# One program for the linear attention and the feed-forward, 512 tokens at a time

## The chip, the cores and the metric

The kernel runs on one core of a Trainium2 chip. The time is that of one execution on the device, in microseconds; the median of the runs shown is 2300.51 us. The profile is of one execution, taken by the hardware profiler; its instants are counted from the first instruction (the span's start).

## What is computed

Two layers, each of three parts with a residual, on x of 32 x 64 tokens x 256, all in float32. The change touches the second and third part of layer 0:

```python
x = x + L0_xattn(ctx, layernorm(x))            # latent attention, untouched
x = x + L0_attn(layernorm(x))                  # linear attention
x = x + L0_ffn(layernorm(x))                   # gated feed-forward
x = x + L1_xattn(layernorm(x), ctx, ctx, mask) # from here on: the decoder, untouched
x = x + L1_attn(layernorm(x))
x = x + L1_ffn(layernorm(x))
```

The linear attention takes xn = layernorm(x), q = relu(xn Wq + bq), k = relu(xn Wk + bk), v = xn Wv + bv, and for each sequence of 64 tokens and each of 16 heads of width 16 the state k^T v and the sum of k. The context is q times the state over max(q times the sum, 1e-6). Then y = context + xn goes through a layer norm of its own with gamma and beta. The feed-forward is silu(h Wg) * (h Wu), then Wd, with 768 hidden columns and weights given as integers, which are scaled by 1/127.

## The kernel before

The 2048 tokens are 16 tiles of 128 (NT); a chunk (CH) is 512 tokens, four tiles, and there are four chunks (NCH). x lies in SBUF all the time as x_sb, one row a token. The program is a list of stages (STAGES): latent_attention, linear_attention, feed_forward, then the decoder. Each stage has one instruction stream for each engine, written out by hand, with semaphores between them; nothing reorders them. Between two stages stands end_stage: the semaphores are cleared and all engines meet at a barrier, so no work of a stage begins ahead of the end of the one before. DMAs are issued by SyncE at the head of each stage.

Both stages begin with NormTranspose: statistics of all 16 tiles on VectorE (gather, L107), seven small steps on all 16 columns (L109 to L117), the power -0.5 on GpSimd (L125), 16 normalised tiles on VectorE (L128), transposes on TensorE (L192) and copies on ScalarE (L205); the feed-forward also subtracts the rounded copy (L176) for a low part.

linear_attention then computes all queries (L280, ScalarE L331) and goes through the tiles in the order keys_values(0), then for each t: states(t), keys_values(t+1), contexts(t). A tile's matmuls are keys and values (L289), states (L300) and contexts (L312). Its vector work is the two bias additions (L350, L351), the masked states (L362, L364), and the denominators, the division and the addition of xn into y (L372 to L382). ScalarE has the Relu of the keys (L337). PSUM has one bank for keys and values, two for states, one for contexts. Behind the last tile stand the statistics of y (L107 again), the power, and the scaling of 16 tiles with gamma and rstd (L397, L401). GpSimd adds beta to x_sb in one instruction (L263).

feed_forward loads the integer weights, converts them on VectorE (L495, L497), rounds them to fp32r on ScalarE (L475, L478) and takes the low parts on GpSimd (L441, L443). A product is then three fp32r matmuls (PASSES: high times high, high times low, low times high), by product3 (L83). For each chunk and each of 6 groups of 128 hidden columns (NH): gate and up matmuls into two banks each, Silu on ScalarE (L485), the product on VectorE (L514), rounding on ScalarE (L489), the low part on VectorE (L516). Then down for four tiles (L468) into two banks, and the addition to x_sb on VectorE (L504).

In the attention TensorE waits as follows: states(t) for the keys and values of t in SBUF and for the states of t-1 to be read out; keys_values(t+1) for the values of t to be read out; contexts(t) for the masked states of t, and for y of t-1.

TileStats, the decoder's form of the statistics, works on four tiles (PER) at a time: L540, L547 to L555, L564. The decoder's first 512-column matmuls are at L845.

## Time and profile before

| | us |
|---|---|
| median of three runs | 2300.51 (2300.44 to 2300.74) |
| profiled execution | 2298.4 |
| its span | 2296.7 |
| start of linear_attention (first SyncE issue) | 911.72 |
| start of feed_forward (first SyncE issue) | 1030.22 |
| start of the decoder (first SyncE issue) | 1171.61 |

Over the whole span TensorE is busy for 2145.7 us (93%), VectorE 1202.0 (52%), ScalarE 1066.5 (46%), GpSimd 483.7 (21%). These shares are means over very different stages. The page's 40 slices of 57.4 us show it: in slices 16 to 19 (861 to 1091 us) TensorE's digits are 7, 8, 4 and 5, where nearly all others are 9, and the digit of the granted clock falls to 7 in two of them. So the stages have to be read one by one: the stretches give the engines' busy time and the granted clock (1.00 is 2.4 GHz, 0.50 is 1.2 GHz), the timeline gives the order of the instructions and what each waited for.

### The profile page before, as it was taken

The numbers are of one execution on the slowest core, as the hardware profiler recorded it, in microseconds if no ns is written. First come the engines' busy times: TensorE is split into PE (matmuls) and PEld (weight loads), VectorE is DVE, ScalarE is ACT, GpSimd is POOL, SyncE is SP. The second block draws the span as 40 slices with busy tenths as digits, with TensorE's granted clock in tenths as the row PEclk, the third lists the DMA queues.
The fourth block names the chain that finished last, engine by engine and source line by source line (L and its number), as shares of the span: only waits on it lengthen the run. The fifth ranks groups of instructions, "written<-read, shape, count | busy, mean of one in ns | idle before, by whom it ended". The sixth has DMA issues, their size and how long they took to land. (4 is left out here: it accounts for less than half of the span.)

```text
span 2296.7 us, 51145 instructions
## 1 busy us (share of the span) xinstructions
PE 2145.7 (93%) x21377; PEld 1876.0 (82%) x21377; DVE 1202.0 (52%) x3545; ACT 1066.5 (46%) x2411; POOL 483.7 (21%) x365
## 2 busy tenths in 40 slices
PE   6999999999999997845979999999999899999999
PEld 6888989898988896424857888878989889898898
DVE  6655555555555554485345778862786532313311
ACT  4545444545444543203226666653444344444443
POOL 1000000000000000102011212223454454545544
PEclk9999999999999998977989999998999999999999
DMA  4100000000000000000031111010101011011000
GB/s 138 29 20 15 20 15 20 15 20 20 15 20 15 20 2 21 4 11 31 1 102 30 31 30 30 12 39 1 56 1 38 1 38 37 1 38 37 1 10 28
DMA packets 48805, 58.12 MB, mean 25 GB/s; under 512 B 6529, under 2 KB 40129, under 8 KB 48449
## 3 DMA queue, kind: packets, MB, share of 16 engines
q1 hardware_dynamic: 48576, 54.85, 7.6%
q8 instruction: 171, 2.80, 0.5%
q14 instruction: 58, 0.47, 0.1%
HBM read 46.72 MB, written 2.10 MB: 21 GB/s over the span
## 5 line engine op out<-in xcount | busy, mean ns | idle before, releaser
L797 POOL TENSOR_TENSOR moe_h<-moe_hr,moe_h 128x512 fp32r<-128x512 f32 x256 | 361.4, 1412 | 428.0 <-ACT moe_hr L1109 428.0
L1108 ACT ACTIVATE moe_h<-bank,dec_b 128x512 fp32r<-128x512 f32 x256 | 176.4, 689 | 418.9 <-PE bank L83 415.8
L2092 DVE TENSOR_REDUCE lat_neg_max<-bank 128x1 f32<-128x320 f32 x256 | 113.6, 486 | 319.0 <-PE bank L1873 319.0
L83 PE MATMUL bank<-lat_wv,lat_kv_t 128*128 128x256 f32 (+1 forms) x1728 | 264.8, 303 | 10.3 <-ACT lat_v L1967 3.9
L83 PE MATMUL bank<-lat_kv_t,lat_wk 128*128 128x320 f32 x1536 | 256.3, 316 | 0.0
L83 PEld LDWEIGHTS bank<-lat_wv,lat_kv_t 128*128 128x128 f32 x1728 | 224.1, 190 | 33.7 <-ACT lat_v L1967 5.7
L83 PEld LDWEIGHTS bank<-lat_kv_t,lat_wk 128*128 128x128 f32 x1536 | 225.8, 188 | 0.1
L1463 DVE SCALAR_TENSOR_TENSOR x_sb<-bank,moe_xs,x_sb 128x256 f32<-128x256 f32 x96 | 39.8, 477 | 352.0 <-PE bank L966 351.9
L83 PE MATMUL bank<-dec_xt,dec_lo 128*128 128x512 f32 x512 | 202.6, 396 | 0.0
L1981 ACT ACTIVATE lat_p<-bank,lat_neg_max 128x320 f32<-128x320 f32 x256 | 137.0, 535 | 114.0 <-DVE lat_neg_max L2092 114.0
L1569 POOL TENSOR_TENSOR lat_rs_rstdc<-lat_rs_varc,lat_rs_halfc 128x4 f32<-128x4 f32 x16 | 16.2, 1014 | 765.8 <-DVE lat_rs_varc L1561 765.8
L966 PE MATMUL bank<-dec_hi,moe_h 128*128 128x256 f32 x1024 | 166.5, 285 | 9.0 <-DVEq L1489 6.1
L1109 ACT ACTIVATE moe_hr<-bank,dec_b 128x512 f32<-128x512 f32 x256 | 174.6, 682 | 0.0
L1967 ACT COPY lat_v<-bank 128x512 f32<-128x512 f32 x128 | 75.1, 587 | 211.0 <-PE bank L83 211.0
L966 PEld LDWEIGHTS bank<-dec_hi,moe_h 128*128 128x128 f32 x1024 | 151.0, 193 | 21.4 <-issue 6.5
L966 PE MATMUL bank<-moe_hi,moe_h 128*128 128x256 f32 x1024 | 163.9, 282 | 3.0 <-POOL moe_h L797 2.9
L966 PE MATMUL bank<-dec_lo,moe_h 128*128 128x256 f32 x1024 | 164.8, 283 | 0.0
L83 PE MATMUL bank<-dec_xt,dec_hi 128*128 128x512 f32 x512 | 163.2, 400 | 0.0
L966 PEld LDWEIGHTS bank<-moe_hi,moe_h 128*128 128x128 f32 x1024 | 148.5, 189 | 14.9 <-POOL moe_h L797 4.6
L83 PE MATMUL bank<-dec_xt,moe_hi 128*128 128x512 f32 x512 | 159.4, 392 | 0.0
L1062 ACT ACTIVATE att_p<-att_sc,att_low 128x256 f32<-128x256 f32 x256 | 113.2, 510 | 83.7 <-DVE att_low L1216 83.7
L966 PEld LDWEIGHTS bank<-dec_lo,moe_h 128*128 128x128 f32 x1024 | 140.5, 190 | 0.0
(316 smaller groups left out, 3954.3 us busy)
## 6 DMA issues: line engine op xcount, KB each, us to landing
raw_w<-in_L_ffn_W SPq DMA_DIRECT2D x16, 1024.0 KB, 6.5
lat_ctx_raw<-in_ctx SPq DMA_DIRECT2D x16, 512.0 KB, 4.1
att_ctx_raw<-in_ctx_turned SPq DMA_DIRECT2D x16, 512.0 KB, 3.8
lat_kv_t<-lat_lt SPq DMA_DIRECT2D x32, 128.0 KB, 2.2
out_x<-x_sb SPq DMA_DIRECT2D x4, 512.0 KB, 2.9
x_sb<-in_x SPq DMA_DIRECT2D x1, 1792.0 KB, 14.7
lat_xl_now<-lat_xl SPq DMA_DIRECT2D x7, 256.0 KB, 4.5
lat_raw<-in_L_xattn_Wq SPq DMA_DIRECT2D x1, 1024.0 KB, 7.5
```

The source lines that it names most:

```text
L83: mm = pe.matmul(out, lhs(a, k), rhs(b, k), start=first and k == 0 and n == 0, stop=last and k == KD - 1 and n == 2)
L797: pool.tensor_tensor(h[:, g % 2, 1, :], hr[:, g % 2, :], h[:, g % 2, 0, :].bitcast(F32), ALU.subtract).then_inc(h_lo, 1)
L966: mm = pe.matmul(y_bank[c % 2 * 2 + i // 2][:, i % 2 * D:(i % 2 + 1) * D], h[:, n % 2, b, i * P:(i + 1) * P], w2(e % 2, a)[:, at, :], star ...
L1062: act.activation(p[:, m, r, :], sc[:, m, r, :], ACT.Exp, bias=low[:, m, r:r + 1], scale=-1.0).then_inc(p_ready, 1)
L1108: act.activation(h[:, n % 2, 0, :], h_bank[n % 2][:, :], ACT.Relu, bias=bias).then_inc(h_hi, 1)
L1109: act.activation(hr[:, n % 2, :], h_bank[n % 2][:, :], ACT.Relu, bias=bias).then_inc(h_f, 1)
L1463: dve.scalar_tensor_tensor(out=x_sb[:, t, :], in0=src(t), scalar=xs[:, t, e:e + 1], in1=x_sb[:, t, :], op0=ALU.mult, op1=ALU.add).then_inc ...
L1569: pool.tensor_tensor(self.rstd[:, :], self.vareps[:, :], self.half[:, :], ALU.pow).then_inc(self.rstd_ready, 1)
L1967: act.copy(v[:, vp % 2, 2 * b:2 * b + 2, :].rearrange("p t n -> p (t n)"), bank_of("v", c, off, a)[:, :]).then_inc(v_done, 1)
L1981: act.activation(p[:, hp % 2, h * LK:(h + 1) * LK], s_bank[h][:, 0:LK], ACT.Exp, bias=neg_max[:, u:u + 1], accum_out=rsum[:, u:u + 1]).the ...
L2092: dve.tensor_reduce(neg_max[:, u:u + 1], s_bank[h][:, 0:LK], AX.X, ALU.max, negate=True).then_inc(s_max, 1)
```

## The change

linear_attention and feed_forward become one stage, linear_feed; one barrier goes. Work goes by chunks of 512 tokens, and the feed-forward of chunk c-1 stands between the pieces of the attention of chunk c:

- TensorE: for each piece i of 0 to 4 a gate/up pair of the chunk before (gate_up), contexts of tile i-1, states of tile i, keys and values of tile i+1; then the sixth pair, the next chunk's transposes and queries, and the four downs, with the next keys and the transposes for this chunk's feed-forward between them. Chunk 0's attention has no feed-forward beside it, and the feed-forward of chunk 3 stands alone at the end.
- The eight PSUM banks are shared out anew: one for gate, one for up (before: two each), two for down, one for keys and values, two for states, which serve both kinds of transposes and the queries too, one for contexts.
- Statistics by TileStats, four tiles at a time, three of them (l, y, f). The normalised tiles are now made on ScalarE (Identity with scale rstd and bias shift, where shift is -mean times rstd, a new small multiply on GpSimd) instead of VectorE. Each chunk's transposes go four to a bank, with copies and subtractions of 512 columns.
- The integer weights are converted on GpSimd instead of VectorE (two tensor_scalar instructions); the low parts stay on GpSimd. All of it stands in one queue with the powers and with beta, which is added four tiles at a time. The weights' DMAs are issued at the head of the merged stage behind those of the attention.
- down waits for all six low parts at its first tile (before: one by one).

The order of each engine, cut (first the statistics, then GpSimd, TensorE, ScalarE, VectorE):

```diff
-        self.half = tools.sb("st_half" + tag, [P, n])
+class TileStats:
+
+
+
+    PER = 4
+
+    def __init__(self, tools, stats, rstd_ready, tag, double=False, minus=False):
+        self.raw = tools.sb("ts_raw" + tag, [P, NT, 6])
+        self.tmp = tools.sb("ts_tmp" + tag, [P, 5, NT])
+        self.mean = tools.sb("ts_mean" + tag, [P, NT])
+        self.vareps = tools.sb("ts_var" + tag, [P, NT])
+        self.rstd = tools.sb("ts_rstd" + tag, [P, NT])
+        self.half = tools.sb("ts_half" + tag, [P, NT])
         self.stats, self.rstd_ready = stats, rstd_ready
-        self.steps = n + 7
-
-    def gather(self, dve, row, base):
-
-        n, raw, tmp = self.n, self.raw, self.tmp
-        for t in range(n):
-            dve.bn_stats(raw[:, t, :], row(t)).then_inc(self.stats, 1)
-        dve.wait_ge(self.stats, base + n)
+        self.steps = self.PER + 7
+        self.half_sum = -0.5 if minus else 0.5
+        self.gain, self.bias = (1.0 + EPS, EPS * EPS) if double else (1.0, EPS)
+
+    def row(self, dve, src, t):
+        dve.bn_stats(self.raw[:, t, :], src).then_inc(self.stats, 1)
+
...
+        dve.tensor_scalar(tmp[:, 4, :], tmp[:, 2, :], self.gain / D, self.bias, ALU.mult, ALU.add).then_inc(self.stats, 1)
+        dve.wait_ge(self.stats, base + 6)
+        dve.scalar_tensor_tensor(out=self.vareps[:, at], in0=tmp[:, 3, :], scalar=0.25 * self.gain, in1=tmp[:, 4, :],
                                  op0=ALU.mult, op1=ALU.add).then_inc(self.stats, 1)
 
...
+            def power_and_shift(norm, shift, ready, c):
+
+                at = slice(c * PER, (c + 1) * PER)
+                norm.power(pool, c)
+                pool.wait_ge(norm.rstd_ready, c + 1)
+                pool.tensor_tensor(shift[:, at], norm.mean[:, at], norm.rstd[:, at], ALU.mult).then_inc(ready, 1)
+
+            def add_beta(c):
+                pool.wait_ge(l_xn, PER * (c + 1))
+                at = slice(c * PER, (c + 1) * PER)
+                pool.tensor_tensor(x_sb[:, at, :], x_sb[:, at, :], beta[:, :].unsqueeze(1).to_broadcast([P, PER, D]),
+                                   ALU.add).then_inc(x_beta, 1)
+
+            def low_weights_up():
+                pool.wait_ge(gu_hi, 1)
+                pool.tensor_tensor(wgu[:, 1], wf[:, :], wgu[:, 0].bitcast(F32), ALU.subtract).then_inc(gu_lo, 1)
+
+            def low_weights_down():
+                pool.wait_ge(wd_hi, 1)
+                pool.tensor_tensor(wd[:, 1], wdf[:, :], wd[:, 0].bitcast(F32), ALU.subtract).then_inc(wd_lo, 1)
+
+            power_and_shift(norm_l, shift_l, l_shift, 0)
+            pool.wait_ge(ffn_loads, 48)
+            pool.tensor_scalar(wf[:, :], wi[:, :], 1.0 / 127.0, None, ALU.mult).then_inc(gu_float, 1)
             pool.wait_ge(loads, 128)
-            pool.wait_ge(front.xn_ready, NT)
-            pool.tensor_tensor(x_sb[:, :, :], x_sb[:, :, :], beta[:, :].unsqueeze(1).to_broadcast([P, NT, D]),
-                               ALU.add).then_inc(beta_added, 1)
-            pool.wait_ge(consts, 3)
-            norm2.power(pool, 0)
+            add_beta(0)
+            pool.tensor_scalar(wdf[:, :], wdi[:, :], 1.0 / 127.0, None, ALU.mult).then_inc(wd_float, 1)
+            low_weights_up()
+            power_and_shift(norm_l, shift_l, l_shift, 1)
+            norm_y.power(pool, 0)
+            power_and_shift(norm_f, shift_f, f_shift, 0)
+            low_weights_down()
+            for c in range(1, NCH):
+                add_beta(c)
+                if c + 1 < NCH:
+                    power_and_shift(norm_l, shift_l, l_shift, c + 1)
+                norm_y.power(pool, c)
+                power_and_shift(norm_f, shift_f, f_shift, c)
...
+            def turn_rows(c):
+                pe.wait_ge(l_xn, PER * (c + 1))
+                if c >= 1:
+                    pe.wait_ge(state_ready, 4 * PER * c)
+                for i in range(PER):
+                    for kd in range(KD):
+                        mm = pe.transpose(st_bank[i // 2][:, (2 * kd + i % 2) * P:(2 * kd + i % 2 + 1) * P],
+                                          xn[:, c % 2, i, kd * P:(kd + 1) * P], k.ident[:, :])
+                    if i % 2:
+                        mm.then_inc(l_psum, 1)
+
+            def queries(c):
+                pe.wait_ge(l_xt, 2 * c + 2)
+                for m in range(KD):
+                    for kd in range(KD):
+                        mm = pe.matmul(st_bank[m][:, :], wq[:, kd, m * P:(m + 1) * P], xt[:, kd, :],
+                                       start=kd == 0, stop=kd == KD - 1)
...
+            def turn_ffn(c):
+                pe.wait_ge(f_xn, PER * (c + 1))
+                pe.wait_ge(q_done, KD * min(c + 2, NCH))
+                pe.wait_ge(state_ready, 4 * PER * (c + 1))
+                for i in range(PER):
+                    for kd in range(KD):
+                        mm = pe.transpose(st_bank[i // 2][:, (2 * kd + i % 2) * P:(2 * kd + i % 2 + 1) * P],
+                                          fn[:, i, kd * P:(kd + 1) * P], k.ident[:, :])
+                    if i % 2:
+                        mm.then_inc(f_psum, 1)
+
+            def gate_up(c, h):
+                n = c * NH + h
+                if n == 0:
+                    pe.wait_ge(gu_lo, 1)
+                if h == 0:
+                    pe.wait_ge(f_lo, 2 * c + 2)
+                for g, (bank, done, freed) in enumerate(((gate_bank, gate_psum, silu_done), (up_bank, up_psum, h_done))):
+                    if n >= 1:
+                        pe.wait_ge(freed, n)
+                    product3(pe, bank[:, :], lambda a, kd: wgu[:, a, kd, g, h * P:(h + 1) * P],
+                             lambda a, kd: ft[:, a, kd, :]).then_inc(done, 1)
+
+            def down(c, i):
+                n = c * PER + i
+                if n == 0:
+                    pe.wait_ge(wd_lo, 1)
+                if n >= 2:
+                    pe.wait_ge(x_done, n - 1)
+                if i == 0:
+                    pe.wait_ge(h_lo, NH * (c + 1))
+                for h in range(NH):
+                    for j, (a, b) in enumerate(PASSES):
+                        mm = pe.matmul(down_bank[n % 2][:, 0:D], ht[:, a, h, i * P:(i + 1) * P], wd[:, b, h, :],
...
+            turn_rows(0)
+            pe.wait_ge(loads, 128)
+            queries(0)
             keys_values(0)
-            for t in range(NT):
-                states(t)
-                if t + 1 < NT:
-                    keys_values(t + 1)
-                contexts(t)
+            for c in range(NCH):
+                for i in range(PER + 1):
+                    if c >= 1:
+                        gate_up(c - 1, i)
+                    if i >= 1:
+                        contexts(PER * c + i - 1)
+                    if i < PER:
+                        states(PER * c + i)
+                    if i + 1 < PER:
+                        keys_values(PER * c + i + 1)
+                if c >= 1:
+                    gate_up(c - 1, NH - 1)
+                if c + 1 < NCH:
+                    turn_rows(c + 1)
+                    queries(c + 1)
+                if c >= 1:
+                    down(c - 1, 0)
+                    down(c - 1, 1)
+                if c + 1 < NCH:
+                    keys_values(PER * (c + 1))
+                if c >= 1:
+                    down(c - 1, 2)
+                turn_ffn(c)
+                if c >= 1:
+                    down(c - 1, 3)
+            for h in range(NH):
+                gate_up(NCH - 1, h)
+            for i in range(PER):
+                down(NCH - 1, i)
...
+            def rows_apply(c):
+                act.wait_ge(l_shift, c + 1)
+                for i in range(PER):
+                    t = PER * c + i
+                    act.activation(xn[:, c % 2, i, :], x_sb[:, t, :], ACT.Identity, bias=shift_l[:, t:t + 1],
+                                   scale=norm_l.rstd[:, t:t + 1]).then_inc(l_xn, 1)
+
+            def rows_turned(c):
+                if c >= 1:
+                    act.wait_ge(kv_psum, PER * c)
+                for half in range(2):
+                    act.wait_ge(l_psum, 2 * c + half + 1)
+                    act.copy(xt[:, :, half * 2 * P:(half + 1) * 2 * P],
+                             st_bank[half][:, :].rearrange("p (k n) -> p k n", k=KD)).then_inc(l_xt, 1)
+
+            def queries(c):
+                for m in range(KD):
+                    act.wait_ge(q_psum, KD * c + m + 1)
+                    act.activation(qt[:, c % 2, m, :], st_bank[m][:, :], ACT.Relu, bias=bq[:, m:m + 1]).then_inc(q_done, 1)
+
+            def keys(t):
...
+            def ffn_apply(c):
+                act.wait_ge(f_shift, c + 1)
+                act.wait_ge(x_lin, PER * (c + 1))
+                for i in range(PER):
+                    t = PER * c + i
+                    act.activation(fn[:, i, :], x_sb[:, t, :], ACT.Identity, bias=shift_f[:, t:t + 1],
+                                   scale=norm_f.rstd[:, t:t + 1]).then_inc(f_xn, 1)
+
+            def ffn_turned(c):
+                for half in range(2):
+                    act.wait_ge(f_psum, 2 * c + half + 1)
+                    act.copy(ft[:, 0, :, half * 2 * P:(half + 1) * 2 * P],
+                             st_bank[half][:, :].rearrange("p (k n) -> p k n", k=KD)).then_inc(f_hi, 1)
+
...
+            rows_apply(0)
+            rows_turned(0)
+            act.wait_ge(loads, 128)
+            queries(0)
+            keys(0)
+            for c in range(NCH):
+                for i in range(PER + 1):
+                    if c >= 1:
+                        gate(c - 1, i)
+                        high(c - 1, i)
+                    if i + 1 < PER:
+                        keys(PER * c + i + 1)
+                    if c == 0 and i == 0:
+                        act.wait_ge(gu_float, 1)
+                        act.copy(wgu[:, 0], wf[:, :]).then_inc(gu_hi, 1)
+                    if c == 0 and i == 2:
+                        act.wait_ge(wd_float, 1)
+                        act.copy(wd[:, 0], wdf[:, :]).then_inc(wd_hi, 1)
+                    if i == PER - 1 and c + 1 < NCH:
+                        rows_apply(c + 1)
+                if c >= 1:
+                    gate(c - 1, NH - 1)
+                    high(c - 1, NH - 1)
+                if c + 1 < NCH:
+                    rows_turned(c + 1)
+                    queries(c + 1)
+                ffn_apply(c)
+                if c + 1 < NCH:
+                    keys(PER * (c + 1))
+                ffn_turned(c)
+            for h in range(NH):
+                gate(NCH - 1, h)
+                high(NCH - 1, h)
...
+            def scale_rows(c):
+
+                dve.wait_ge(norm_y.rstd_ready, c + 1)
+                dve.wait_ge(x_beta, c + 1)
+                for i in range(PER + 2):
+                    t = PER * c + i
+                    if i < PER:
+                        dve.scalar_tensor_tensor(out=y[:, i, :], in0=y[:, i, :], scalar=norm_y.mean[:, t:t + 1],
+                                                 in1=gamma[:, :], op0=ALU.subtract, op1=ALU.mult).then_inc(scaled, 1)
+                    if 1 <= i <= PER:
+                        dve.wait_ge(scaled, t)
+                        dve.scalar_tensor_tensor(out=x_sb[:, t - 1, :], in0=y[:, i - 1, :], scalar=norm_y.rstd[:, t - 1:t],
+                                                 in1=x_sb[:, t - 1, :], op0=ALU.mult, op1=ALU.add).then_inc(x_lin, 1)
+                    if i >= 2:
+                        dve.wait_ge(x_lin, t - 1)
+                        norm_f.row(dve, x_sb[:, t - 2, :], t - 2)
+                norm_f.close(dve, c)
...
-                                             in1=x_sb[:, t - 1, :], op0=ALU.mult, op1=ALU.add).then_inc(x_done, 1)
+            for c in range(NCH):
+                for i in range(PER + 1):
+                    t = PER * c + i
+                    if c >= 1:
+                        hidden(c - 1, i)
+                    if i >= 1:
+                        contexts(t - 1)
+                    if i < PER:
+                        states(t)
+                    if i + 1 < PER:
+                        keys_values(t + 1)
+                    if i >= 1:
+                        y_row(t - 1)
+                    if i == 0 and c + 1 < NCH:
+                        rows_stats(c + 1)
+                    if i == 1 and c + 1 < NCH:
+                        norm_l.close(dve, c + 1)
+                    if i == PER:
+                        norm_y.close(dve, c)
+                    if c >= 1:
+                        hidden_low(c - 1, i)
+                if c >= 1:
+                    hidden(c - 1, NH - 1)
+                    hidden_low(c - 1, NH - 1)
+                scale_rows(c)
+                if c >= 1:
+                    residual(c - 1, 0)
+                    residual(c - 1, 1)
+                if c + 1 < NCH:
+                    keys_values(PER * (c + 1))
+                if c >= 1:
+                    residual(c - 1, 2)
+                ffn_low(c)
+                if c >= 1:
+                    residual(c - 1, 3)
+            for h in range(NH):
+                hidden(NCH - 1, h)
+                hidden_low(NCH - 1, h)
+            for i in range(PER):
...
```

## Rows read from the trace of the kernel before

**Rows 1.** stretches of the trace: us, busy of each engine (instructions), granted clock, DMA
```profile
911.72:1030.22 118.50, 74.62 (x384) 36.83 (x384) 75.86 (x270) 18.12 (x40) 15.10 (x7) 0.82 0.05 12
...
1030.22:1171.61 141.39, 111.73 (x608) 94.52 (x608) 67.18 (x121) 40.28 (x67) 14.97 (x4) 0.87 0.05 17
...
946.00:1006.30 60.30, 51.92 (x320) 26.03 (x318) 44.78 (x175) 6.67 (x16) 0.00 (x0) 0.99 0.00 1
...
1006.30:1065.00 58.70, 8.29 (x31) 4.79 (x32) 45.92 (x113) 7.77 (x15) 14.35 (x4) 0.50 0.12 40
...
1065.00:1168.00 103.00, 101.30 (x563) 87.80 (x562) 40.01 (x64) 32.51 (x52) 3.54 (x1) 0.99 0.00 1
```

**Rows 2.** timeline around the tiles: start, us, engine, line, instruction
```profile
911.75 5.32 DVE L107 BATCH_NORM_STATS2 lin_st_raw<-x_sb 128x6 f32<-128x256 f32 x16 [1.31 <-PEq L2210]
...
918.22 2.90 POOL L125 TENSOR_TENSOR lin_st_rstd<-lin_st_var,lin_st_half 128x16 f32<-128x16 f32 x1 [6.11 <-DVE lin_st_var L117]
...
1016.41 0.88 DVE L397 SCALAR_TENSOR_TENSOR lin_y<-lin_y,lin_st_meany,lin_gamma 128x256 f32<-128x256 f32 x2 [3.09 <-POOL lin_st_rstdy L125]
```

**Rows 3.** timeline, one attention tile, 961.9 to 966
```profile
961.92 0.69 PE L312 MATMUL bank<-lin_kvm,lin_qt 128*64 128x136 f32 x8
...
962.03 0.42 DVE L350 TENSOR_TENSOR lin_kpre<-bank,lin_bkv 128x256 f32<-128x256 f32 x1 [0.67 <-PE bank L289]
...
962.49 0.42 ACT L337 ACTIVATE lin_kk<-lin_kpre 128x256 f32<-128x256 f32 x1 [3.19 <-DVE lin_kpre L350]
...
962.96 0.72 PE L300 MATMUL bank<-lin_vext,lin_kk 64*128 64x129 f32 x8 [0.34 <-ACT lin_kk L337]
...
963.61 1.98 PE L289 MATMUL bank<-lin_wkv,lin_xt 128*128 128x512 f32 x4
...
965.63 0.42 DVE L350 TENSOR_TENSOR lin_kpre<-bank,lin_bkv 128x256 f32<-128x256 f32 x1 [0.67 <-PE bank L289]
```

**Rows 4.** timeline, the last feed-forward chunk
```profile
1144.80 16.03 PE L83 MATMUL bank<-ffn_xt,ffn_wgu 128*128 128x512 f32 x68
...
1161.64 0.62 ACT L489 CAST ffn_ht<-ffn_hf 128x512 fp32r<-128x512 f32 x1 [1.58 <-DVE ffn_hf L514]
...
1163.05 7.09 PE L468 MATMUL bank<-ffn_wd,ffn_ht 128*128 128x256 f32 x57 [0.42 <-DVE ffn_ht L516]
```

**Rows 5.** timeline, transposes and eight passes of 512 after an idle stretch
```profile
1054.32 1.09 PE L192 MATMUL bank<-ident,ffn_xn 128*128 128x128 f32 x4 [11.49 <-DVE ffn_xt L176]
...
1182.51 5.39 PE L845 MATMUL bank<-rows_a,att_wq 128*128 128x512 f32 x8 [0.36 <-DMA att_bo<-in_L_xattn_bo]
...
1186.45 0.19 PEld L845 LDWEIGHTS bank<-rows_a,att_wq 128*128 128x128 f32 x1 [0.24 <-issue]
```

**Rows 6.** lines alone (ns min/median/max), then a group by line
```profile
L128 DVE TENSOR_SCALAR ffn_xn<-x_sb,ffn_st_mean,ffn_st_rstd x16: 401/404/6877, 1041.2 to 1052.6; 128x256 f32<-128x256 f32 x16
...
L516 DVE TENSOR_TENSOR ffn_ht<-ffn_hf,ffn_ht x24: 692/692/843, 1070.5 to 1162.3; 128x512 fp32r<-128x512 f32 x24
...
L441 POOL TENSOR_TENSOR ffn_wgu<-ffn_wf,ffn_wgu 128x3072 fp32r<-128x3072 f32 x1 | 6.9, 6858 | 2.8 <-ACT ffn_wgu L475 2.8
```

**Rows 7.** groups by line, GpSimd: busy us, mean ns, idle before, releaser
```profile
L263 POOL TENSOR_TENSOR x_sb<-x_sb,lin_beta 128x4096 f32<-128x4096 f32 x1 | 8.8, 8843 | 5.4 <-DVE lin_xn L128 5.4
...
L564 POOL TENSOR_TENSOR dec_ts_rstda<-dec_ts_vara,dec_ts_halfa 128x4 f32<-128x4 f32 x4 | 4.8, 1192 | 14.4 <-DVE dec_ts_vara L555 14.4
```

**Rows 8.** timeline, and DMA issues by line (KB, us to landing)
```profile
915.13 0.43 SPq L251 DMA_DIRECT2D lin_beta<-in_L_attn_beta  x1
...
lin_beta<-in_L_attn_beta SPq DMA_DIRECT2D x1, 128.0 KB, 5.1
...
ffn_wdi<-in_L_ffn_w_down SPq DMA_DIRECT2D x1, 768.0 KB, 8.2
```

**Rows 9.** groups by line, ScalarE: busy us, mean ns
```profile
L475 ACT CAST ffn_wgu<-ffn_wf 128x3072 fp32r<-128x3072 f32 x1 | 2.8, 2759 | 38.7 <-DVE ffn_wf L495 38.7
...
L485 ACT ACT_TABLE_LOAD x1 | 1.3, 1283 | 0.0
```

419 lines of the change are left out of this document (122 added, 297 removed).

## The prediction

> **What bounds the kernel now.** I read the stretches first. The two stages that the change merges take 118.5 us (linear attention) and 141.4 us (feed-forward), 259.9 us of the 2296.7 us span; TensorE is busy for only 74.6 and 111.7 us of them, at a mean granted clock of 0.82 and 0.87 [rows 1]. Nothing else of the program changes. Two stretches keep TensorE busy. In the sixteen tiles of the attention (946 to 1006.3) TensorE shows 51.9 of 60.3 us busy, but at 0.99 clock and with short matmuls whose results are awaited one by one; in the feed-forward proper (1065 to 1168) it is busy for 101.3 of 103 us: dense work. Outside both lie 34 us ahead of the tiles and the 58.7 us between the last tile and the first gate matmul, in which TensorE is busy for 8.3 us and VectorE for 45.9: work over all sixteen tiles at once, statistics (16 in 5.32 us), the small steps that close them (the power on GpSimd starts 1.15 us after the last of the 16, and takes 2.9 us for 16 columns), the scaling (0.40 us a piece, 32 pieces) [rows 2].
>
> The timeline of one tile says what bounds the sixteen. Its keys' addition starts at 962.03, ScalarE's Relu 962.49, the state matmuls 962.96, the next tile's key/value matmuls 963.61, and the next addition 965.63: a ring of 3.60 us in which each engine waits for the one before [rows 3]. VectorE is idle for 0.67 us of each, which is its play. A piece of feed-forward between two steps of this ring costs what it costs TensorE, while it hides the latencies.
>
> **TensorE's work at the high clock, per 512 tokens.** Gate and up: 68 matmuls in 16.03 us, so 72 in 16.8 (last latency off). Down: 57 in 7.09, so 72 in 8.6 [rows 4]. Queries: 8 passes at a pitch of 0.43 us, 3.4 [rows 5]. Keys and values: 4 tiles x 4 passes x 0.43 = 6.9. States and contexts: 0.65 + 0.70 a tile from the starts in [rows 3], 5.4. Turning 4 tiles: four transposes took 1.09 us at a clock of 0.5 [rows 1, 5], so eight take about 1.0 at full clock; there are two such groups a chunk, 2.0. Sum 43.1 us; four chunks 172 us, against 259.9 now. The best case is thus not below some 185 us, with a front that no matmul fills.
>
> **The front, from the start of the merged stage to the first gate matmul.** Four rows of statistics and their closing 2.3 us; power 1.2 [rows 7] and the new shift multiply, for which no row stands (between nothing and the power's own 1.2; 0.4 taken, since it has four elements): 4.0. ScalarE applies four tiles at 0.41 (its 128x256 pass in [rows 3]): 5.7. Eight transposes at the low clock and two copies: 8.4. The eighth load is issued 3.4 us in and lands 5.1 us later [rows 8]: about 9. The same shape of eight passes from an idle engine took 5.39 us at the decoder's start, four at the low clock's pitch and then 0.43 [rows 5]: queries until 14.4. From a tile's keys to its row of y are two ring periods, so 7.2 + 3 x 3.6 = 18.0; the four statistics of the next chunk and their closing stand in the first two pieces on VectorE and cost about 1.5 beyond its play: 34.
>
> Here GpSimd matters. Its queue now holds the int-to-float conversions that VectorE did, then beta, then the low weights, all ahead of the powers of the next chunk and of y. The feed-forward loads are issued behind the eight others, 3.9 to 4.9 us in; the last took 8.2 us [rows 8]: 13.1. The conversion of 3072 has no row; its ends are half of beta's rate (one stream for two, 3.3 us) and the same size with two inputs, 6.9 [rows 6, 7]; 4.6 taken: 17.7. Beta for four tiles is a quarter of 8.84: 19.9; the second conversion 2.3: 22.2. ScalarE's high weights (2.76 us [rows 9]) come after the keys of tile 1, until 23.8; then the low ones hold GpSimd for 6.9 us, until 30.7. The trace shows what that does to VectorE: during this same instruction one tensor_scalar between SBUF tiles took 6877 ns where its neighbours took 404, while a subtraction with two SBUF inputs under the other GpSimd subtraction stretched only from 692 to 843 [rows 6]. The closing of the next chunk's statistics has two such tensor_scalars and stands at 25.7 in VectorE's order, so all of VectorE's queue (the next contexts, states and keys) waits behind it until 30.7: +5. Price range 0 (were four elements not held) to 6.9.
>
> The Trainium skill, GPSIMD Engine Reference, section Key points, says that GpSimd shares its SBUF interfaces with VectorE, with contention for instructions in a 2-port perf mode or with two SBUF inputs. By the rule, read as a full hold, each addition into y would be held as well; the sum would grow by at most the 6.9 us once more. The 843 ns say that two inputs share instead of waiting.
>
> Then y is complete at about 40, its closing and power 42.3; scaling 8 x 0.40 and the new statistics 4 x 0.33: 46.8; closing, power, shift 49.3; applied 51.0; turned, copied (0.6), low part (0.7): 53.7. The turn and queries of chunk 1 and the next key/value matmuls lie inside this wait. The one Silu table load [rows 9] falls before the first Silu and is hidden under the gate matmuls. **Front 53.7 us.**
>
> **A merged chunk.** A slot is one gate/up pair (2.8 us), the contexts of one tile, the states of the next, the keys of the one after: 5.87 us of TensorE. VectorE in a slot: the attention's part 2.93 (a period less the 0.67 idle of [rows 3]), y statistics 0.33, the product and the low part 0.69 each (one shape, [rows 6]) = 4.7; ScalarE three passes of 0.4 to 0.6 us. Laid out, the product for slot n is ready 0.8 us after its up matmuls; the one PSUM bank for gate and the one for up are asked for again over 2 us later; the states' evictions come 2.3 us ahead of their contexts. So TensorE decides, and giving up the double banks costs nothing. Slots of a chunk: 16.8 + 5.2 (three key/value groups) + 5.4 = 27.4.
>
> Behind the sixth pair, at 0: VectorE finishes the sixth product, rounded on ScalarE, at 2.8; scaling until 7.3, closing 8.2, GpSimd 9.7, ScalarE 11.4. TensorE turns the next chunk's rows until 1.0, and must wait for two copies behind the rounding in ScalarE's queue, until 3.4; queries 6.9, two downs 11.2, key/values 12.9, down 15.1, feed-forward turn 16.1, down 18.3; its copies and low part are there at 17.6. Stall 2.5. **Chunks 1 and 2: 27.4 + 18.3 = 45.7 us each.**
>
> Chunk 3 has no next rows to turn: down waits for the low part at 2.8, two are done at 7.1; the third needs the first residual, which stands behind the scaling and closing (8.6) on VectorE: 10.8; turn at 11.5 to 12.5; down 14.7. **42.1 us.**
>
> The last feed-forward stands alone: 16.8; all downs now wait for the last low part (2.2 us after the last up matmul; before, only the last of six steps waited), then 8.6, last addition 0.5: **28.2 us**; the barrier to the decoder, 1.0, as now.
>
> **Sum.** 53.7 + 2 x 45.7 + 42.1 + 28.2 + 1.0 = 216.4, against 259.9: 43.5 us less. The profiled execution has 2298.4 us around a span of 2296.7; it becomes 2254.9. The median shown, 2300.5, stands 2.1 above that execution: 2257.0.
>
> **Rivals.**
> - *No hold in the front.* Tiny tensor_scalars slip past GpSimd: 5 us less, 2252. For it: they are four elements long, and no row has one beside a long GpSimd instruction. Chance 0.20.
> - *The slots run in series.* If an engine's order makes the attention ring start only when the pair is done, a slot takes 2.8 + 3.6 = 6.4 instead of 5.87, by twelve slots 6.4 us, and the ends of three chunks lengthen by as much as their scaling chain, about 4 us each: 2275. For it: VectorE at 4.7 of 5.87 is in strict order, and takes 5.6 where a closing is added; GpSimd's beta (2.2 us a chunk) can eat the play. Chance 0.25.
> - *Activation tables alternate.* Only three table loads stand in the whole trace, 1283 ns each, the second before the first Silu [rows 9]; after Silu only copies follow until the decoder's exponentials, so no row shows Relu or Identity under Silu's table. Two loads a slot are 2.6 us of latency against 2 of play: 0.6 x 12, and about 1.3 at each chunk's end: 2268. Chance 0.04. The Trainium skill, ScalarE: Activation LUTs, section Table sets, says that cheap functions such as relu, copy and identity are in every set; by that rule this case doesn't occur.
> - *Slower: the clock.* From the last attention tile to the first gate matmul, with TensorE nearly idle, the granted clock was 0.50 [rows 1], and the first four passes after an idle stretch ran at half rate [rows 5]. If the three merged chunks (128 us of matmuls) ran at the low level, 1.2 GHz, they would take 128 us more: 2385. It decides at 43.5/128, a third of this work at the low level. Against it: the attention tiles, with more gaps than the slots will have, ran at 0.99 [rows 1]. Chance 0.03.
> - *The change doesn't do what it says:* the overlap arises but leaves under 0.2%. Only a stall as long as the gain would do it; 0.01.
>
> The forecast itself has 0.45 (its own range 2253 to 2263: GpSimd's conversion 1.3 less or 2.3 more, states and contexts 0.35 a tile less, the closings a little held by powers); 0.02 is for a time below 2246.
>
> **Range and chances.** From the no-hold case with dense states (2246) to just above the case in series (2277). Faster by over 0.2% (about what a measurement of this kernel can tell from no change): 0.96; within: 0.01; slower: 0.03.
>
> **What would show it.** Right: a merged stage of about 216 us; first gate matmul 50 to 56 us in; a closing tensor_scalar of several us beneath the low-weights subtraction; slots of 5.9 us with TensorE at clock 1.0; starts of consecutive chunks 45 to 46 us apart; no more than three table loads. Wrong: slots of 6.4 us or more with TensorE waiting for VectorE; a front over 60 us because a power stands behind GpSimd's weights; a clock below 0.9 in the merged chunks; a wait for the loads ahead of the queries well beyond 9 us.

## The result, and the profile after

The changed kernel takes 2268.11 us (median of four runs, 2261.45 to 2268.70), the kernel before 2300.48 on the same chip: ratio 0.9856, with a 95% interval of 0.9836 to 0.9876. That is 32.4 us or 1.4% faster. 2257.0 was forecast, with a range of 2246 to 2277: the sign is right, and 11 us of the expected gain of 43.5 did not come.

The profiled execution took 2267.77 us, its span is 2266.0 (2296.7 before). The merged stage begins with its first SyncE issue at 912.74 and ends where the decoder begins, at 1140.08. These are its stretches: us, then busy time and instructions of TensorE, its weight loads, VectorE, ScalarE and GpSimd, then the granted clock, the DMA share and GB/s.

```profile
912.74:1140.08 227.34, 192.06 (x992) 137.09 (x992) 136.30 (x412) 71.17 (x123) 47.68 (x33) 0.89 0.06 17
912.74:972.68 59.94, 35.65 (x125) 17.90 (x125) 34.68 (x100) 19.35 (x30) 31.19 (x18) 0.71 0.20 62
972.68:1019.63 46.95, 45.04 (x248) 33.02 (x249) 31.08 (x102) 16.66 (x31) 7.33 (x7) 0.97 0.00 1
1019.63:1066.81 47.18, 45.27 (x251) 32.46 (x250) 31.51 (x103) 16.35 (x30) 6.55 (x6) 0.96 0.00 1
1066.81:1109.24 42.43, 39.24 (x231) 30.21 (x229) 28.65 (x90) 11.71 (x21) 2.60 (x3) 0.96 0.00 1
1109.24:1140.08 30.84, 26.86 (x146) 23.51 (x144) 10.39 (x17) 7.11 (x12) 0.00 (x0) 0.94 0.00 1
```

The first row stands against the first two of [rows 1]: 227.34 us for 118.50 and 141.39, so 32.5 less; outside the stage the span became 1.9 us longer. In chunks 1 and 2 TensorE is now busy for 96% of the time (92% in chunk 3) at a clock of 0.96 or 0.97; the two gaps of [rows 1] (the head of the stage and the stretch from 1006.3 to 1065 with TensorE busy for 8.3 of 58.7 us) have become one, the front, at a clock of 0.71.

| stretch | forecast | measured |
|---|---|---|
| front, to the first gate matmul | 53.7 | 59.94 |
| chunk 1 | 45.7 | 46.95 |
| chunk 2 | 45.7 | 47.18 |
| chunk 3 | 42.1 | 42.43 |
| last feed-forward and barrier | 29.2 | 30.84 |
| stage | 216.4 | 227.34 |

So 6.2 of the missing 10.9 us lie in the front. Its timeline (start, us, engine, line, instruction, and in brackets the idle time before it and what ended it), of GpSimd, and of what VectorE did at the same time:

```profile
922.80 6.22 PE L272 MATMUL bank<-body_xt,body_wq 128*128 128x512 f32 x8 [2.16 <-DMA body_beta<-in_L_attn_beta]
...
928.82 7.96 POOL L238 TENSOR_SCALAR body_wf<-body_wi 128x3072 f32<-128x3072 int32 x1 [12.31 <-DMA body_wdi<-in_L_ffn_w_down]
...
935.15 1.40 DVE L107 BATCH_NORM_STATS2 body_ts_rawl<-x_sb 128x6 f32<-128x256 f32 x4
...
936.75 2.36 POOL L225 TENSOR_TENSOR x_sb<-x_sb,body_beta 128x1024 f32<-128x1024 f32 x1
...
937.47 1.92 DVE L513 TENSOR_TENSOR body_y<-body_ctxn,body_xn 128x256 f32<-128x256 f32 x1
939.06 4.27 POOL L241 TENSOR_SCALAR body_wdf<-body_wdi 128x1536 f32<-128x1536 int32 x1
...
940.14 0.41 DVE L482 TENSOR_TENSOR body_kpre<-bank,body_bkv 128x256 f32<-128x256 f32 x1
...
941.14 1.33 DVE L114 TENSOR_TENSOR body_ts_tmpl<-body_ts_rawl 128x4 f32<-128x4 f32 x1
...
942.39 0.15 DVE L115 TENSOR_TENSOR body_ts_tmpl<-body_ts_rawl 128x4 f32<-128x4 f32 x1
...
942.65 0.70 DVE L118 TENSOR_SCALAR body_ts_meanl<-body_ts_tmpl 128x4 f32<-128x4 f32 x1
...
943.31 6.65 POOL L230 TENSOR_TENSOR body_wgu<-body_wf,body_wgu 128x3072 fp32r<-128x3072 f32 x1
943.43 6.54 DVE L122 SCALAR_TENSOR_TENSOR body_ts_varl<-body_ts_tmpl 128x4 f32<-128x4 f32 x1
949.90 0.16 DVE L503 TENSOR_SCALAR body_dmax<-bank 128x16 f32<-128x16 f32 x1
950.05 1.04 POOL L131 TENSOR_TENSOR body_ts_rstdl<-body_ts_varl,body_ts_halfl 128x4 f32<-128x4 f32 x1
...
952.21 1.18 PE L308 MATMUL bank<-body_kvm,body_qt 128*64 128x136 f32 x8 [6.87 <-DVE body_kvm L495]
```

Read the pairs. A VectorE step on four elements a partition (L122) takes 6.54 us, from 0.12 us after the start of GpSimd's subtraction for the low weights to its end; ahead of it the addition into y (L513, 0.42 us otherwise) ends 0.3 us after beta's does. The addition of the bias (L482), which reads PSUM and one SBUF operand, takes its usual 0.41 under GpSimd's second conversion, and the statistics (L107) their 0.35 a tile under the first. Behind L122 TensorE waits 6.87 us for the masked states. Ahead of it two other steps of the closing are held beneath the second conversion, L114 for 1.2 us and L118 for 0.5, while L115 between them, with two SBUF inputs like L114, takes its usual 0.15.

The chunks are as laid out: in a full slot gate/up pairs start 5.96 and 5.94 us apart. Four rows show where the time beyond that went:

```profile
972.68 4.38 PE L83 MATMUL bank<-body_ft,body_wgu 128*128 128x512 f32 x12 [1.65 <-DVE body_ft L546]
...
1004.90 3.70 PE L272 MATMUL bank<-body_xt,body_wq 128*128 128x512 f32 x8 [1.91 <-ACT body_xt L398]
...
1050.38 5.40 PE L272 MATMUL bank<-body_xt,body_wq 128*128 128x512 f32 x8 [1.91 <-ACT body_xt L398]
...
1128.05 10.35 PE L345 MATMUL bank<-body_wd,body_ht 128*128 128x256 f32 x72 [2.30 <-DVE body_ht L561]
```

The first is the first gate/up pair, 2.9 us in the next chunk. The next two are the same eight query passes behind the same wait of 1.91 us, once at the high clock (granted 1.00) and once largely at the low one: granted 1.00 in the first 0.40 us, then 0.50 for most of the rest. The last is the last 72 down matmuls, 8.6 by [rows 4]: granted 1.00 in their first 1.2 us, then 0.50 for a part.

### The profile page after: what moved, and what is told of

The parts are those of the page before. It is cut to its first block and busy times, and to the rows that moved or that the text cites. A ratio compares the mean times of both kernels' runs of the same rounds, so it can differ in the third digit from the quotient of the medians.

```text
span 2266.0 us, 51163 instructions
## 1 busy us (share of the span) xinstructions
PE 2152.0 (95%) x21377; PEld 1881.8 (83%) x21377; DVE 1194.6 (53%) x3566; ACT 1077.4 (48%) x2427; POOL 500.4 (22%) x387
## 5 line engine op out<-in xcount | busy, mean ns | idle before, releaser
L1013 PEld LDWEIGHTS bank<-moe_hi,moe_h 128*128 128x128 f32 x1024 | 148.4, 189 | 14.6 <-POOL moe_h L844 4.2
```

The costliest lines, as they stand in the source:

```text
L1013: mm = pe.matmul(y_bank[c % 2 * 2 + i // 2][:, i % 2 * D:(i % 2 + 1) * D], h[:, n % 2, b, i * P:(i + 1) * P], w2(e % 2, a)[:, at, :], star ...
```

## The experiments

All ratios are to the kernel before, measured beside each. The stretches are those of the profiled execution:

| kernel | median | ratio [95%] | stage | front | chunk 1 | chunk 2 | chunk 3 | last |
|---|---|---|---|---|---|---|---|---|
| changed kernel | 2268.11 | 0.9856 [0.9836, 0.9876] | 227.34 | 59.94 | 46.95 | 47.18 | 42.43 | 30.84 |
| e1_pieces | 2264.14 | 0.9840 [0.9822, 0.9859] | 221.90 | 55.79 | 47.14 | 47.17 | 42.45 | 29.35 |
| e2_close_late | 2260.56 | 0.9832 [0.9816, 0.9848] | 224.81 | 58.60 | 47.24 | 47.17 | 42.45 | 29.35 |
| e3_down_h | 2263.03 | 0.9839 [0.9824, 0.9853] | 223.75 | 59.77 | 48.58 | 45.48 | 42.45 | 27.47 |
| e4_serial | 2345.45 | 1.0213 [1.0189, 1.0237] | 306.43 | 60.87 | | | | |
| e5_one_bank (kernel before) | 2299.27 | 1.0006 [0.9993, 1.0020] | | | | | | |
| e6_conv_dve | 2261.71 | 0.9836 [0.9821, 0.9850] | 223.54 | 56.08 | 46.99 | 47.18 | 42.45 | 30.84 |
| e7_best | 2251.16 | 0.9799 [0.9780, 0.9818] | 213.92 | 53.25 | 46.01 | 44.34 | 42.84 | 27.48 |
| e8_double | 2274.49 | 0.9895 [0.9875, 0.9915] | 234.09 | 66.57 | 47.07 | 47.18 | 42.44 | 30.83 |
| e10_best2 | 2244.87 | 0.9769 [0.9754, 0.9784] | 209.26 | 47.91 | 46.48 | 44.35 | 43.01 | 27.51 |
| e11_fill | 2265.33 | 0.9854 [0.9834, 0.9873] | 226.69 | 61.76 | 47.64 | 45.48 | 42.44 | 29.37 |

The medians of single repairs lie within 5 us of each other, and their intervals overlap with one another's and with the changed kernel's; it is the stretches of one profiled execution each that tell them apart. The front carries a scatter of its own: GpSimd's conversion starts when the last feed-forward load has landed, 15.4 to 17.8 us into the stage, and with no edit to it the front ends 43.9 to 44.0 us after that start (changed kernel 16.08 and 59.94, e3 15.90 and 59.77, e11 17.76 and 61.76).

**e4_serial: is it the interleaving?** The pieces of the feed-forward are taken out of the attention's loop on each engine and stand whole behind it; TensorE's part:

```diff
             for c in range(NCH):
                 for i in range(PER + 1):
-                    if c >= 1:
-                        gate_up(c - 1, i)
                     if i >= 1:
                         contexts(PER * c + i - 1)
...
+                turn_ffn(c)
+                for h in range(NH):
+                    gate_up(c, h)
+                for i in range(PER):
+                    down(c, i)
                 if c + 1 < NCH:
                     turn_rows(c + 1)
                     queries(c + 1)
```

> The changed kernel with one thing taken back: the feed-forward of a chunk stands whole behind that chunk's attention, on every engine, instead of between the pieces of the next. Chunks of 512 tokens, one stage, the same front with GpSimd's conversions and ScalarE's rows, no barrier: all that stays. Theory: the interleaving brings the whole gain and the chunking alone costs. Front 60, last feed-forward 28 behind each of four attentions; an attention alone takes its four periods of 3.6, queries, and the exposed chain of statistics, power, scaling, statistics, power, turn: about 38 us; so 60 + 28 + 3 x 66 = 286 us for the stage against 227.3 now and 259.9 before: about 2327 us (2310 to 2340), slower than the kernel before. Rival: the gain comes from the lost barrier, from rows on ScalarE and from chains that four tiles shorten; then it stays below 2290.

Measured: 2345.45 us, slower than the kernel before by 2.1%. The rival falls: chunks of four tiles, rows on ScalarE and the lost barrier bring no gain by themselves; against the changed kernel the interleaving is worth 79 us of the stage. The stage is 20 us longer than expected, and its rows say why:

```profile
1038.83 1.97 PE L318 MATMUL bank<-ident,body_fn 128*128 128x128 f32 x8 [12.98 <-ACT body_fn L405]
1042.21 19.39 PE L83 MATMUL bank<-body_ft,body_wgu 128*128 128x512 f32 x72 [1.40 <-DVE body_ft L527]
1063.89 10.36 PE L345 MATMUL bank<-body_wd,body_ht 128*128 128x256 f32 x72 [2.30 <-DVE body_ht L542]
```

Each chunk's scaling chain leaves TensorE idle for 12.98 us, the 72 gate/up matmuls behind it take 18.4 to 19.4 us instead of the 16.51 of the changed kernel's last chunk, and the 72 downs 10.36 instead of 8.6. A chunk takes 70.4 to 71.7 us, not 66, and the last feed-forward 32.7, not 28.

**e1_pieces: the long subtraction in eight pieces.** Each piece is one GpSimd instruction of 384 elements, with the first gate matmul waiting for all eight.

```diff
-                pool.tensor_tensor(wgu[:, 1], wf[:, :], wgu[:, 0].bitcast(F32), ALU.subtract).then_inc(gu_lo, 1)
+                for kd in range(KD):
+                    for g in range(2):
+                        for s in range(0, HID, HID // 2):
+                            e = s + HID // 2
+                            pool.tensor_tensor(wgu[:, 1, kd, g, s:e], wf[:, kd, g, s:e],
+                                               wgu[:, 0, kd, g, s:e].bitcast(F32), ALU.subtract).then_inc(gu_lo, 1)
```

> The changed kernel, with the 3072-column low-weights subtraction on GpSimd cut into eight of 384 columns; same work, same place. Theory (one long GpSimd instruction holds a VectorE instruction with two SBUF inputs until it ends): the 6.54 us instruction of the statistics' closing falls under 1.5 us, the closing ends some 5 us earlier, and the front (stage start to first gate matmul, 59.9 us) falls by about 4, to 56, as TensorE's turn and queries of chunk 1 at the low clock come to stand next to the chain; 2264. Rival (the length of GpSimd's queue decides, not the hold): the powers behind the subtraction come no earlier, the front stays 60 within 1 us.

```profile
941.91 8.04 POOL L234 TENSOR_TENSOR body_wgu<-body_wf,body_wgu 128x384 fp32r<-128x384 f32 x8
942.03 0.88 DVE L122 SCALAR_TENSOR_TENSOR body_ts_varl<-body_ts_tmpl 128x4 f32<-128x4 f32 x1
...
943.85 1.24 DVE L518 TENSOR_TENSOR body_y<-body_ctxn,body_xn 128x256 f32<-128x256 f32 x1
```

The closing step takes 0.88 us instead of 6.54: it is held to the end of one piece (8.04 / 8 = 1.0 us), although GpSimd works longer in all (8.04 for 6.65). The front is 4.15 shorter; 0.7 of that is the earlier landing of the loads, 3.4 the edit. The subtraction as a whole ends later than in the changed kernel (37.9 us into the stage for 37.2), so the rival falls: it is the hold on VectorE that counts, and not the length of GpSimd's queue by itself.

**e8_double: the long subtraction twice.** The second gives the same values.

```diff
                 pool.tensor_tensor(wgu[:, 1], wf[:, :], wgu[:, 0].bitcast(F32), ALU.subtract).then_inc(gu_lo, 1)
+                pool.wait_ge(gu_lo, 1)
+                pool.tensor_tensor(wgu[:, 1], wf[:, :], wgu[:, 0].bitcast(F32), ALU.subtract).then_inc(gu_lo, 1)
```

> The changed kernel with the subtraction for the low part of the gate and up weights done twice in a row on GpSimd (the second gives the same values), and the first gate matmul waiting for both. It doubles the one suspected cost. Theory (a VectorE instruction with two SBUF inputs is held to the end of the GpSimd instruction it meets, and the powers queue behind it): one closing step still shows 6.5 us, the next two-input step of VectorE (a closing step or an addition into y) is held as well under the second, and the front grows by 5 to 7 us, to 65 to 67 us: about 2274. Rival (the subtraction lies beside work that sets the front anyway): the front grows by under 1.5 us: 2268 to 2269.

```profile
942.59 6.65 POOL L230 TENSOR_TENSOR body_wgu<-body_wf,body_wgu 128x3072 fp32r<-128x3072 f32 x1
942.72 6.54 DVE L122 SCALAR_TENSOR_TENSOR body_ts_varl<-body_ts_tmpl 128x4 f32<-128x4 f32 x1
...
949.32 6.65 POOL L232 TENSOR_TENSOR body_wgu<-body_wf,body_wgu 128x3072 fp32r<-128x3072 f32 x1
...
950.19 6.06 DVE L515 TENSOR_TENSOR body_y<-body_ctxn,body_xn 128x256 f32<-128x256 f32 x1
```

The second subtraction holds the next instruction with two SBUF inputs, an addition of 256 columns, to its own end (955.97 and 956.25). The front grows by 6.63 us, 0.26 of it by a later landing of the loads, and the stage by 6.75: 6.4 us for an instruction of 6.65, nearly its whole length.

**e2_close_late: the closing of the next chunk's statistics two tiles later,** so that it doesn't meet the subtraction.

```diff
-                    if i == 1 and c + 1 < NCH:
+                    if i == (3 if c == 0 else 1) and c + 1 < NCH:
                         norm_l.close(dve, c + 1)
```

> The changed kernel, with the closing of chunk 1's statistics moved on VectorE from the second to the fourth piece of chunk 0, out of the time of the long subtraction on GpSimd. Theory as predicted (only tensor_scalar-like tiny steps are held, a two-input tensor_tensor merely shares): the hold is gone, the contexts and y of tiles 1 to 3 come 5 us earlier, the front falls from 59.9 to about 54. Rival (each instruction with two SBUF inputs is held to the end): the addition into y of tile 1 takes the hold over with 3 to 5 us, and the front stays between 58 and 61.

```profile
939.44 6.68 POOL L230 TENSOR_TENSOR body_wgu<-body_wf,body_wgu 128x3072 fp32r<-128x3072 f32 x1
943.28 3.11 DVE L513 TENSOR_TENSOR body_y<-body_ctxn,body_xn 128x256 f32<-128x256 f32 x1
...
948.15 0.16 DVE L122 SCALAR_TENSOR_TENSOR body_ts_varl<-body_ts_tmpl 128x4 f32<-128x4 f32 x1
```

The rival stated there was right. The closing slips free (0.16), and the addition into y is held in its place until 946.4. The front is 58.6, not 54. The loads landed 0.8 us later here; counted from the conversion's start the move brought 2.1 us.

**e6_conv_dve: the two conversions back on VectorE,** ahead of and behind keys_values(0).

```diff
-            pool.wait_ge(ffn_loads, 48)
-            pool.tensor_scalar(wf[:, :], wi[:, :], 1.0 / 127.0, None, ALU.mult).then_inc(gu_float, 1)
...
+            dve.wait_ge(ffn_loads, 48)
+            dve.tensor_scalar(wf[:, :], wi[:, :], 1.0 / 127.0, None, ALU.mult).then_inc(gu_float, 1)
             keys_values(0)
+            dve.tensor_scalar(wdf[:, :], wdi[:, :], 1.0 / 127.0, None, ALU.mult).then_inc(wd_float, 1)
```

> The changed kernel, with both int-to-float conversions back on VectorE, in its idle time around the first keys (1.76 and 0.95 us there; 7.96 and 4.27 us on GpSimd), and the rounding of the gate and up weights on ScalarE right behind the first keys. Theory (GpSimd's conversions push its long subtraction onto the tiles and its beta onto y): the subtraction runs from about 22 us after the stage's start instead of 30.6, still holds one addition into y for about 4 us, and the front falls from 59.9 to about 53. Rival (the conversions were hidden, only the subtraction's hold counts and comes the same): front 58 or more.

```profile
929.90 1.76 DVE L570 TENSOR_SCALAR body_wf<-body_wi 128x3072 f32<-128x3072 int32 x1 [13.60 <-DMA body_wdi<-in_L_ffn_w_down]
...
935.27 6.68 POOL L230 TENSOR_TENSOR body_wgu<-body_wf,body_wgu 128x3072 fp32r<-128x3072 f32 x1 [9.18 <-ACT body_wgu L443]
...
938.25 3.97 DVE L509 TENSOR_TENSOR body_y<-body_ctxn,body_xn 128x256 f32<-128x256 f32 x1
```

The conversion takes 1.76 us on VectorE for 7.96 on GpSimd. The subtraction is over 28.0 us into the stage instead of 37.2, 9.2 earlier, but the front gains 3.9 and not 7, between theory (53) and rival (58 or more): the hold now falls on the first tile's y, with three tiles still to come behind it. That this is the whole of the missing 3 us is argued, not shown.

**e3_down_h: down waits for its low parts one by one,** as before the change.

```diff
-                if i == 0:
-                    pe.wait_ge(h_lo, NH * (c + 1))
                 for h in range(NH):
+                    if i == 0:
+                        pe.wait_ge(h_lo, c * NH + h + 1)
```

> The changed kernel, with the wait for the low parts put back to one for each of the six groups in the first down of a chunk. Theory (a wait of 2.3 us ahead of the downs costs itself and then the clock): behind the last chunk the wait falls from 2.3 to about 0.6 and the 72 downs take 8.7 us instead of 10.35, so the last feed-forward with the barrier falls from 30.8 to 27.4; the third chunk (1066.8 to 1109.2, 42.4 us) stays, since its transposes wait for the scaling chain on VectorE, GpSimd and ScalarE. In all 3.4 us less than the changed kernel. Rival (the slow downs have another cause): only the 1.7 us of the wait come back.

```profile
1092.55 2.78 PE L345 MATMUL bank<-body_wd,body_ht 128*128 128x256 f32 x21 [0.76 <-DVE body_ht L561]
1098.26 2.41 PE L345 MATMUL bank<-body_wd,body_ht 128*128 128x256 f32 x18 [2.93 <-DVE x_sb L567]
...
1120.83 1.95 PE L345 MATMUL bank<-body_wd,body_ht 128*128 128x256 f32 x15
1123.21 7.09 PE L345 MATMUL bank<-body_wd,body_ht 128*128 128x256 f32 x57 [0.43 <-DVE body_ht L561]
```

As expected: 27.47 us for 30.84 in the last stretch, the last 57 at the speed of [rows 4]. The wait accounts for 1.9 us of it. The other 1.5 can't be put down to this edit alone, for e1 and e2 took 29.35 in the last stretch with the wait of 2.30 unchanged. Chunk 1 is 1.6 longer than in the changed kernel and chunk 2 1.7 shorter, because here the first group of queries took 5.40 us and the second 3.70. In chunk 3 nothing is gained, because the third down waits 2.93 us for the first residual, which VectorE's order puts behind the scaling.

**e11_fill: is it TensorE's idleness that makes the matmuls behind a short wait slow?** Idle matmuls are put into two kinds of wait; no wait is removed.

```diff
+            def fill(n):
+                for j in range(n):
+                    pe.matmul(kv_bank[:, :], wgu[:, 0, 0, 0, 0:P], ft[:, 0, 0, :], start=True, stop=True)
...
                     turn_rows(c + 1)
+                    if c >= 1:
+                        fill(8)
                     queries(c + 1)
...
                 gate_up(NCH - 1, h)
+            fill(9)
```

> The changed kernel with idle matmuls in two kinds of wait: eight of 128x512 (0.22 us each) between the turn of chunks 2 and 3 and their queries, and nine between the last up block and the last downs. They write into the bank for keys and values, which nobody reads then; no wait is taken away. Theory (in those waits of about 2 us TensorE stands idle and comes back at the low level of its clock, which costs the next matmuls 1.5 to 1.8 us): both eight-pass groups of queries take 3.7 us (3.70 and 5.40 in the changed kernel), the last 72 down matmuls 8.6 to 8.9 instead of 10.35, and the start of these groups doesn't move by more than 0.3 us; stage 223.5 to 224.5 instead of 227.3. Rival (the first matmuls behind such a wait are slow for another reason, such as operands just written): the groups keep 5.40 and 10.35 and the stage stays at 227.

```profile
1051.72 2.09 PE L278 MATMUL bank<-body_ft,body_wgu 128*128 128x512 f32 x8
1053.87 3.70 PE L272 MATMUL bank<-body_xt,body_wq 128*128 128x512 f32 x8
...
1127.39 2.20 PE L278 MATMUL bank<-body_ft,body_wgu 128*128 128x512 f32 x9
1129.86 8.87 PE L349 MATMUL bank<-body_wd,body_ht 128*128 128x256 f32 x72 [0.27 <-DVE body_ht L568]
```

Both query groups take 3.70 us, and the last 72 down matmuls 8.87 instead of 10.35, at the same place. Chunk 2 and the last stretch are 1.70 and 1.47 shorter. The stage as a whole is only 0.65 shorter and not 3 to 4, since in this execution the front is 1.8 longer (the loads came 1.7 us later) and the first gate/up pair took 5.07 us for 4.38; that part of the expectation was missed.

One reservation: without filler the groups were not slow every time, so three fast groups could be chance in part. The other runs count for the theory all the same:

| what TensorE did ahead of the group | slow groups |
|---|---|
| waited 1.91 us, then queries (changed kernel, e1, e2, e3, e6, e8) | 7 of 12 took 5.40, the others 3.70 |
| waited 2.30 us, then 72 downs (changed kernel, e1, e2, e6, e8, e4) | 7 of 9 took 10.35, the others 8.86 |
| waited 0.78 us, then queries (e4, e7, e10) | 0 of 7 |
| waited 0.43 us, then the last 57 downs (e3, e7, e10) | 0 of 3 |
| idle matmuls in the wait (e11) | 0 of 3 |

In e11 itself the wait ahead of chunk 3's first downs was left unfilled (2.64 us), and they were slow, 8.20 us for 54 as in the changed kernel, granted 0.50 for a part of it.

**e5_one_bank: the kernel before with one gate and one up bank.**

```diff
-                        if n >= 2:
-                            pe.wait_ge(freed, n - 1)
-                        product3(pe, bank[n % 2][:, :]
+                        if n >= 1:
+                            pe.wait_ge(freed, n)
+                        product3(pe, bank[0][:, :]
```

Silu and the product read the one bank likewise.

> The kernel before with the second gate bank and the second up bank taken away, as the change does: gate matmuls of group n wait for Silu of group n-1, up matmuls for its product. Theory: the gate bank is asked for again 2.8 us after its last matmul and free after 0.6 to 1.0, so nothing waits: 0 us, within 1 us of 2300.5. Rival: each gate or up block waits for the one before it, 0.5 us in 24 groups: 2312.

Measured 1.0006 [0.9993, 1.0020]: no difference; the feed-forward stage is 142.04 us for 141.39. In the kernel before, the banks given up cost nothing that can be measured; in the changed one no gate/up block behind the first shows a wait of its own.

**e7_best and e10_best2: the repairs together.** e7: e1, e3 and e6; gamma and beta on a semaphore of their own, so that the queries wait for six loads; and ScalarE's copies of the turned rows ahead of the sixth rounding:

```diff
                     gate(c - 1, NH - 1)
-                    high(c - 1, NH - 1)
                 if c + 1 < NCH:
                     rows_turned(c + 1)
+                if c >= 1:
+                    high(c - 1, NH - 1)
+                if c + 1 < NCH:
                     queries(c + 1)
```

> The changed kernel with its exposed parts mended together: conversions of the integer weights on VectorE (in place of GpSimd), the low weights in eight pieces, gamma and beta of the attention counted apart so that the queries wait for six loads alone, down waiting group by group, and ScalarE's copies of the turned rows ahead of the sixth rounding. Theory (what held VectorE and filled GpSimd's queue is gone, the holds are at most one piece long): first gate matmul 45 to 50 us in (59.9 in the changed kernel, 56.1 with the conversions alone), last feed-forward 27.4 instead of 30.8, chunks 1 and 2 up to 1 us shorter each: stage 210 to 214, about 2251 us (2247 to 2256). Rival: the front is set by the chain of attention and statistics whatever GpSimd does, and stays at 55: 2258 or more.

The total and the stage came as expected, but by two misses that offset each other: chunk 2 is 2.8 us shorter where up to 1 was expected, for its queries, now behind a wait of 0.78 us, took 3.70 and not 5.40, and the front (53.25) missed its 45 to 50: the queries start at 8.7 us instead of 10.1, but VectorE's conversion waits for the last of three loads until 16.7 us, ahead of the first keys. e10 takes that up:

```diff
             rows_stats(0)
             norm_l.close(dve, 0)
+            rows_stats(1)
+            norm_l.close(dve, 1)
...
-            dve.wait_ge(ffn_loads, 48)
+            dve.wait_ge(ffn_loads, 32)
```

> The version with all repairs (stage 213.9, first gate matmul 53.3 us in, queries from 8.6 us in) and two more: the statistics and the closing of chunk 1's rows stand right behind those of chunk 0, in the 14 us in which VectorE waits for the loads, with their power on GpSimd ahead of beta; and the weights of down are counted apart, so that the conversion of the gate and up weights waits for two of the three loads. Theory (the front is VectorE's chain from the conversion on: it ran from 16.7 us in, with 1.4 us of statistics and 2.3 us of closing, one step held 0.98, in the first two tiles): conversion 2 to 4 us earlier, 2 to 3.5 us less on VectorE: first gate matmul 47.5 to 50 us in, stage 208 to 211, about 2247 us (2244 to 2250). Rival (TensorE at the low level of its clock sets the front's tiles, not VectorE): 52 to 53, 2250 or more.

```profile
925.31 1.76 DVE L582 TENSOR_SCALAR body_wf<-body_wi 128x3072 f32<-128x3072 int32 x1 [10.06 <-DMA body_wi<-in_L_ffn_w_up]
...
933.12 0.55 DVE L518 TENSOR_TENSOR body_y<-body_ctxn,body_xn 128x256 f32<-128x256 f32 x1
```

All as expected: the conversion starts 14.6 us in, no addition into y is held for more than about 0.2, the front is 47.91 and the stage 209.26. The time is 2244.87 us, 2.3% under the kernel before and 0.9% under the changed one (by the two ratios, whose intervals are apart). The last feed-forward runs at a granted clock of 1.00.

## Why the prediction was right, and where 11 us went

**What bounds the kernel, and the gain.** Right. The kernel before lost its time in stretches in which TensorE waited; e4 shows that without the interleaving the same work is 79 us slower than with it. By the time alone two rivals would have fitted better than the forecast, alternating tables (2268) and slots in series (2275); it is the trace that rules them out. No table alternated (three loads in the whole program, one ahead of the first Silu), no slot ran in series (5.95 us, 5.87 forecast, 6.4 by the rival), the clock in the chunks was 0.96 to 0.97, and the single banks cost nothing (e5). Of the prediction's own signs of being right, three failed: the stage (about 216 us; 227.34), the first gate matmul (50 to 56 us in; 59.94) and the chunks' starts (45 to 46 apart; 46.95 and 47.18).

**The front: the hold was there, on another step, and the prices were too low.** A closing step held beneath the low-weights subtraction was forecast at 5 us and is there with 6.4; the rival without a hold falls. But the forecast had put the hold on the two tensor_scalars of the closing (L118, L120) and let steps with two SBUF inputs go free. The step held was L122, which has two; the tensor_scalars stood ahead of the subtraction. By its own reading of the rows nothing would have been held there, so that the term nearly fits is luck in part. Three terms were short. The loads: 9 us for the eight, 10.06 measured, and 13.1 for the feed-forward's, 16.08 measured: eleven loads share the queues where before three stood alone [rows 8]. The conversion on GpSimd: 4.6 taken between ends of 3.3 and 6.9; it took 7.96, above both ends, and the second 4.27 for 2.3. And the low weights were let start behind ScalarE's rounding, when by the forecast's own times the second conversion ended at 22.2 and the rounding at 23.8; so the second conversion had 1.6 us of room, and with the true sizes it is GpSimd's queue that decides when the hold ends: 16.08 + 7.96 + 2.36 + 4.27 + 6.65 = 37.3 us, where 30.7 was forecast. These 6.6 us are the front's error of 6.2; the tail from there to the first gate matmul was forecast at 23.0 and took 22.7. (The forecast's tail has a slip in it: 34 and 5 make 39 us for the complete y, where it went on from about 40.) e8 confirms that the path runs through this subtraction, with 6.4 us for its 6.65.

**A step that was wrong.** "The 843 ns say that two inputs share instead of waiting." They don't. The row was read from minimum and maximum alone; the timeline of the kernel before shows where the one long instance lay:

```profile
1067.31 3.54 POOL L443 TENSOR_TENSOR ffn_wd<-ffn_wdf,ffn_wd 128x1536 fp32r<-128x1536 f32 x1 [16.42 <-ACT ffn_wd L478]
...
1070.54 0.84 DVE L516 TENSOR_TENSOR ffn_ht<-ffn_hf,ffn_ht 128x512 fp32r<-128x512 f32 x1 [0.69 <-ACT ffn_ht L489]
```

It began 0.31 us before the GpSimd instruction ended and so can't show sharing. It was held like the others, for the little that was left: it ended 0.53 us behind the subtraction, 0.16 less than its own 0.69, as the held additions into y of 0.42 us end 0.3 behind theirs. In the changed kernel the additions into y and the two-input closing step L122 were held to the end of the GpSimd subtraction or addition they met (e1, e2, e8). The Trainium skill, SBUF — State Buffer, section SBUF: two separate sides, says this outright: the port pair that GpSimd and VectorE share is an exclusive lock for the whole instruction of the one that starts first, against VectorE instructions in a 2-port mode or with two SBUF inputs, with the latter only if the GpSimd instruction reads SBUF. The trace agrees for GpSimd's subtractions and additions: 6.54 and 6.06 us for steps of 0.16 and 0.42, and 0.41 for one that reads PSUM. For the int-to-float conversion of 1536 it does not: L114 met it and was let go 0.86 us before it ended, L115 and L116 then passed with two SBUF inputs in 0.15 each, and L118 was held again, to its end at 943.33. The release at 0.85 or 0.86 us before the end stands in e1, e3, e8 and e11 too (there behind a hold of 3.17 us). What the conversion does at that point is open. The prediction had weighed the Trainium skill's shorter wording (GPSIMD Engine Reference, section Key points) and put the row above it.

The sum by the rule had been said to grow by at most 6.9 us. Besides L122 the held steps were 1.5 us at beta, 1.2 at L114 and 0.5 at L118. All three lie ahead of the subtraction; its end was set by GpSimd's queue and the tail behind it took no longer than forecast, so they did not lengthen the front.

**The chunks.** The slots were right within 0.1 us each. Chunk 1 is 1.25 over because its first pair took 4.38 us (2.9 at the high clock), chunk 2 1.48 because its queries took 5.40 instead of 3.70. The granted clock fell to 0.50 in the wait of 1.65 us ahead of the pair, and 0.4 us behind the wait of 1.91 ahead of the queries. The forecast had reckoned the queries' stall (2.5; 1.91 measured) and then the high clock behind it. Chunk 3 (42.43 for 42.1) was right in its length. Its third down's wait for the residual, forecast at 1.5 us, shows in e1:

```profile
1092.76 4.55 PE L350 MATMUL bank<-body_wd,body_ht 128*128 128x256 f32 x36 [2.63 <-DVE body_ht L566]
1098.38 2.41 PE L350 MATMUL bank<-body_wd,body_ht 128*128 128x256 f32 x18 [1.07 <-DVE x_sb L572]
```

In the changed kernel the first two downs ran in part at the low clock (8.20 us for three, behind a wait of 2.62) and filled it.

**The last feed-forward.** 2.30 us of wait for the last low part was forecast (2.2), 8.6 us of down matmuls were not: 10.35. That is the 1.6 us over, by the same term. The clock (1.5, 1.7 and 1.75 us) makes 4.95 us, all of the 4.7 by which the parts behind the front were too short. That TensorE's idleness in the wait is the cause is borne out by e11 and the table there; what decides whether a wait of 2 us costs 1.7 us or nothing is not settled, for the same wait gave both.

**Outside the stage** 1.9 us more stand in the profiled execution, 1.0 of it ahead of the stage, in code that no edit touches; the start of the stage lies between 907.8 and 914.0 in the profiled executions here. That is scatter, and it is as large as the effect of a single repair, so that single repairs can be read only from stretches that begin and end inside the stage.

## What to carry to other kernels

When work moves to GpSimd, price it twice: its own length on that engine (4.5 times VectorE's for an integer conversion here), and each VectorE instruction with two SBUF inputs that it will hold, however small (to the end of a two-input GpSimd instruction in every case here); cut long GpSimd instructions into pieces, or put them where VectorE reads PSUM or waits. The hold ends when the queue gets there: sum the queue's whole chain from the load that starts it. And before an outlier in a minimum/maximum row is used as a price, look in the timeline at how much of it overlapped what is blamed.

## What the runs showed of the hardware that was not expected

- A GpSimd tensor_scalar from int32 to float32 takes 2.6 ns an element (7.96 us for 3072), the same on VectorE 0.57 (1.76 us). With two float inputs GpSimd took 2.2 (6.65 us for 3072).
- The hold works the other way too. In the kernel before, a GpSimd power of 16 columns took 4.47 us (1036.73 to 1041.20) where its two fellows took 2.90 and 2.91; VectorE's conversion of 1.76 us had begun 2.66 us behind it and ended 0.05 us ahead of it. No run was made on this.
- Eight pieces of a GpSimd subtraction cost 8.04 us for 6.65: 0.2 us for each extra instruction.
- In or shortly behind waits of 1.6 to 2.6 us TensorE's granted clock sometimes fell to 0.50 (1.2 of 2.4 GHz), which cost up to 1.75 us, and sometimes not: the queries and downs behind such a wait began at 1.00 and the clock fell 0.2 to 1.4 us later. No row of the kernel before had shown that for so short a wait.
- ScalarE's Identity with a pointer for scale and for bias took 0.59 us for 128x256 (2.07 for four), where its Relu took 0.42.
- The landing of the last of eleven loads varied from 15.3 to 17.7 us after the first issue, and the front with it.
